# The last 512 tokens' sends to their expert slots: eight in a row behind one tile, or two behind each of four tiles

## The chip, the cores and the metric

The kernel runs on one core of one Trainium2 chip. The metric is device time in microseconds (us) of one execution, as the median of several. The names of the engines are those of the profile: PE is TensorE, PEld its weight loads, DVE is VectorE, ACT is ScalarE, POOL is GpSimd, SP is SyncE, and SPq is the queue on which SP issues its DMAs.

## The reference

One transformer block over 2048 tokens of width 128, in float32:

```python
h = _layernorm(x) * (1 + ca) + sa
x = x + ga * attention(h)      # 16 query heads, 4 key/value heads of 64, rotary, causal softmax
h = _layernorm(x) * (1 + cb) + sb
x = x + gb * ffn(h)            # 8 experts, 128 -> 512 -> 128, silu(g) * u; the top 2 of 8 for each token
```

The reference computes all eight experts for every token and weighs them with `tok_w`, which is zero but for two of them. The kernel computes only the two that count, so it has to sort tokens by expert.

## The kernel before, in words

Attention fills most of the time. It runs over four key/value groups; each handles the 16 token tiles (128 tokens each) in four chunks of 512 tokens. Then comes the expert stage, the only one that the change touches.

**Slots.** Every token has two rows to be computed, one per chosen expert. Each row is sent to a place in the DRAM tensor `sent`, so that each *slot tile* of 128 rows belongs to one expert. There are 40 slot tiles (`SLOT_TILES`), k = 0 to 39. They are fetched four at a time, as *quads* 0 to 9.

**Two batches of tokens.** The first 12 token tiles (`EARLY`) are ready while attention on the last chunk still runs; their 24 sends go out then, and they fill slot tiles 0 to 15 (`EARLY_SLOTS` is 16). The last four token tiles, 512 tokens, come late: their attention output is normalised, routed and counted between slot tiles 0 and 8 (the `late(k)` steps on PE and DVE), and DVE writes their places, `slot_of`, at slot tile 8 and signals `slots_ready`. Their rows may land in any slot tile from 16 on. A send is one indirect DMA of 128 rows issued by POOL; a token tile has two, one for each choice, so the late batch has eight.

**The work on one slot tile k.** PE does `gate_up(k)` (six matmuls, L1460). ACT takes silu of one half (L839), DVE multiplies it with the other (L1250). PE transposes the product, `turn_hidden(k)` (L1471), ACT copies it out (L832), and PE does `down(k)` (eight matmuls, L1482). DVE weighs the result, `y_out(k)` (L1218), which signals `y_copied`, and POOL writes it to the DRAM tensor `made` with one indirect DMA, `send_back(k)` (L681). PE's order within step k is `gate_up(k)`, `down(k-2)`, `turn_hidden(k-1)`; DVE's is the product of k, then `y_out(k-2)`; POOL's step k begins with `send_back(k-2)`. All queues are in order.

**A new quad.** SP fetches quad q (L549) once the buffer is free. Quad 4, the first that can hold late rows, has one more wait, for all sends to have landed:

```python
if q == EARLY_SLOTS // TB:
    sp.wait_ge(scattered, 2 * TILES * 16)
fetch(q)
```

Then PE transposes the quad (`turn_rows(q)`, L1448), ACT scales and rounds it (L823, L825), POOL computes the low parts (`split_rows(q)`, L675), and only then can PE start `gate_up` on its first tile. For quads 1, 2, 3 and 5 to 9 this begins two or three slot tiles ahead of need. Quad 4 alone is turned in step 15, directly ahead of slot tile 16.

**POOL's order** around the change is steps 8 to 15 of one loop. The sends of the late batch stand in step 10 (`LATE_SEND`), behind `send_back(8)`, all eight ahead of `send_back(9)`; `split_rows(4)` stands in step 15, behind `send_back(13)`.

Of the kernel before, what the change touches and what calls it, by code (L numbers as in the profile page):

```python
# [63 lines left out]
def block_kernel(nc, x_in, Wq, bq, Wk, bk, Wv, bv, Wo, bo, gate, w1, w2, w3, c, wmod,  # L64
# [5 lines left out]
    TILES = T // P  # L70
# [12 lines left out]
    EARLY, EARLY_LOWS = TILES - TB, 3  # L83
# [7 lines left out]
    def weight(x):  # L91

        if x[0] in ("s", "max"):
            _, J, m, t, b = x if x[0] == "max" else (x[0], x[1], x[4], x[3], x[2])
            part = 1.0 if b < J % N_J // PAIRS else ((t + 1) if x[0] == "max" else (TB - t)) / TB
            return part * (3.78 if x[0] == "max" else 2.0)
        if x[0] == "gap":
            return x[1]
        return {"pv": 2.1, "qmax": 1.5, "proj": 3.0, "low": 3.0, "qk": 3.5, "poolsum": 0.01, "maxed": 0.25,
                "diagsum": 3.3, "quadsum": 0.01, "sum": 2.8, "rowsum": 12.6, "norm": 2.8, "modulation": 0.0,  # L100
                "out": 8.0, "ln_stats": 1.0, "ln_scale": 1.0, "ln_turn": 2.0, "router": 4.0, "count": 4.0, "send": 1.0,
                "weights": 1.0}[x[0]]
# [63 lines left out]
    def merge(*placed):  # L166
        return [x for _, x in sorted((y for items in placed for y in items), key=lambda y: y[0])]
# [55 lines left out]
    for g in range(GROUPS):  # L223
        order = group_order(*(next_group if g < GROUPS - 1 else last_pair))
        at = [(p + g * begin[end], x) for (p, _), x in zip(order, of_group([x for _, x in order], g))]
        placed.append(at)
# [51 lines left out]
    with ExitStack() as ctx:  # L278
# [211 lines left out]
        def quad_turn(k):  # L490

            if k == EARLY_SLOTS - 1:
                return EARLY_SLOTS // TB
            q = k // TB + 1
            return q if k % TB == 1 and q < QUADS_OF_SLOTS and q != EARLY_SLOTS // TB else None
# [5 lines left out]
        LATE_OUT, LATE_TURN, LATE_ROUTER, LATE_COUNT, LATE_SEND = 0, 3, 4, 7, 10  # L501
# [75 lines left out]
        def _(pool):  # L577
# [78 lines left out]
            def send(t):  # L656
                late = t >= EARLY
                pool.wait_ge(slots_ready, 1 + late)
                pool.wait_ge(cleared, 16)
                tiles, rows = BATCH[late]  # L660
                for choice in range(2):
                    nc.gpsimd.indirect_dma_start(sent.ap(), bass.IndirectOffsetOnAxis(ap=slot_of[:, choice, t:t + 1], axis=0),  # L662
                                                 rows[:, t - tiles[0], :], None).then_inc(scattered, 16)
# [8 lines left out]
            def split_rows(q):  # L672
                width = len(quad_tiles(q)) * P
                pool.wait_ge(x_rounded, q + 1)
                nc.gpsimd.tensor_tensor(h_parts[:, q % 2, 1, 0:width], hT_full[:, q % 2, 0:width],  # L675
                                        h_parts[:, q % 2, 0, 0:width].bitcast(F32), ALU.subtract).then_inc(x_split, 1)

            def send_back(k):
                pool.wait_ge(y_copied, k + 1)
                pool.wait_ge(back_ready, k // TB + 1)  # L680
                nc.gpsimd.indirect_dma_start(made.ap(), bass.IndirectOffsetOnAxis(ap=back_to[:, k:k + 1], axis=0),  # L681
                                             y_rows[:, k % Y_ROWS, :], None).then_inc(written[k % Y_ROWS], 16)

            split_rows(0)
            for k in range(SLOT_TILES):
                if k >= 2:
                    send_back(k - 2)
                if k == LATE_SEND:
                    for t in range(EARLY, TILES):
                        send(t)  # L690
                if quad_turn(k) is not None:
                    split_rows(quad_turn(k))
            send_back(SLOT_TILES - 2)
# [868 lines left out]
```

## Time and profile before

| what | value |
|---|---|
| time, median of 3 | 1218.36 us (1216.64 to 1220.63) |
| the profiled execution: its own time | 1220.18 us |
| the profiled execution: its span | 1218.3 us |
| mean granted TensorE clock | 0.96 |
| PE busy | 1094.7 us, 90% of the span |
| DVE, POOL, ACT busy | 855.2 us (70%), 602.5 us (49%), 552.7 us (45%) |
| expert stage, first `gate_up` to the end of the span | about 1060 to 1218.3 us |

Positions are counted in microseconds from the start of the span. The span leaves out 1.9 us of the profiled execution's own time. The expert stage is the last 158 us; the stretch at issue lies between 1100 and 1130 us.

### The profile page before, as it was taken

The numbers are of one execution on the slowest core, as the hardware profiler recorded it, in microseconds if no ns is written. First come the engines' busy times: TensorE is split into PE (matmuls) and PEld (weight loads), VectorE is DVE, ScalarE is ACT, GpSimd is POOL, SyncE is SP. The second block draws the span as 40 slices with busy tenths as digits, with TensorE's granted clock in tenths as the row PEclk, the third lists the DMA queues.
The fourth block names the chain that finished last, engine by engine and source line by source line (L and its number), as shares of the span: only waits on it lengthen the run. The fifth ranks groups of instructions, "written<-read, shape, count | busy, mean of one in ns | idle before, by whom it ended". The sixth has DMA issues, their size and how long they took to land.

```text
span 1218.3 us, 16645 instructions
## 1 busy us (share of the span) xinstructions
PE 1094.7 (90%) x5718; PEld 660.7 (54%) x5718; DVE 855.2 (70%) x1751; ACT 552.7 (45%) x1156; POOL 602.5 (49%) x645
## 2 busy tenths in 40 slices
PE   2589999999999999999999999999999897287993
PEld 2355555554565655545656555556555443276893
DVE  3657878777779787777787877677877784664333
ACT  1344444545455445444454454535544344153451
POOL 2743655746346456453465554454555238325341
PEclk9699999999999999999999999999999898589997
DMA  9000000000000000000000000000100010502104
GB/s 240 1 1 1 1 2 1 1 1 1 1 2 1 1 1 1 1 1 1 1 1 1 1 1 1 1 1 1 70 1 1 1 48 32 148 14 75 33 24 119
DMA packets 32209, 25.28 MB, mean 21 GB/s; under 512 B 8448, under 2 KB 27264, under 8 KB 32128
## 3 DMA queue, kind: packets, MB, share of 16 engines
q1 hardware_dynamic: 22528, 17.08, 4.8%
q0 software_dynamic: 2304, 4.79, 1.2%
q10 hardware_dynamic: 7296, 2.36, 0.9%
q8 instruction: 47, 0.77, 0.3%
q14 instruction: 34, 0.28, 0.1%
HBM read 15.68 MB, written 8.54 MB: 20 GB/s over the span
## 4 chain that ended last, share of the span: by engine, by line
PE 71%; DVE 10%; issue 7%; POOL 6%; DMA 3%; ACT 2%; ACTq 1%; SPq 1%; POOLq 0%; DVEq 0%
PE PS L1386 18%; PE PS L1340 12%; PE PS L1368 10%; PE PS L1370 9%; PE PS L1460 4%; PE PS L1316 3%; DVE part_max L984 3%; PE PS L1482 2%; PE PS L1422 2%; PE PS L1353 2%; PE PS L1323 2%; PE PS L1396 2%; POOL sent L662 2%; DVE full L1000 1%; POOL full L616 1%
## 5 line engine op out<-in xcount | busy, mean ns | idle before, releaser
L984 DVE TENSOR_REDUCE part_max<-PS 128x1 f32<-128x512 f32 (+2 forms) x576 | 340.2, 618 | 135.1 <-PE PS L1340 111.2
L764 ACT ACTIVATE full<-PS 128x512 f32<-128x512 f32 x384 | 223.4, 598 | 196.6 <-PE PS L1370 185.5
L1368 PE MATMUL PS<-store 128*128 128x512 f32 (+3 forms) x640 | 273.6, 428 | 10.7 <-ACT full L764 7.2
L1340 PE MATMUL PS<-store 128*128 128x512 f32 (+3 forms) x640 | 249.6, 416 | 2.4 <-DVE V L965 1.3
L1370 PE MATMUL PS<-store 128*128 128x512 f32 (+3 forms) x640 | 234.8, 367 | 0.0
L616 POOL TENSOR_TENSOR full<-full 128x512 f32<-128x512 f32 x128 | 164.2, 1314 | 137.0 <-PE PS L1386 136.0
L773 ACT ACTIVATE diag<-PS 128x512 f32<-128x512 f32 (+3 forms) x256 | 111.3, 441 | 211.2 <-PE PS L1373 179.3
L644 POOL TENSOR_TENSOR lower<-lower 128x320 f32<-128x320 f32 x64 | 60.2, 941 | 275.1 <-DVE lower L962 272.8
L1340 PEld LDWEIGHTS PS<-store 128*128 128x128 f32 x640 | 119.1, 192 | 138.0 <-DVE part_max L984 59.6
L1386 PE MATMUL PS<-full,V 128*64 128x512 f32 x768 | 191.3, 608 | 0.0
L1368 PEld LDWEIGHTS PS<-store 128*128 128x128 f32 x640 | 123.5, 193 | 86.1 <-ACT full L764 28.4
L625 POOL TENSOR_TENSOR full<-full,diag 128x512 f32<-128x512 f32 (+3 forms) x128 | 108.8, 888 | 58.8 <-ACT diag L773 52.5
L1370 PEld LDWEIGHTS PS<-store 128*128 128x128 f32 x640 | 122.2, 191 | 13.2
L744 ACT ACTIVATE store<-PS 128x512 fp32r<-128x512 f32 (+1 forms) x192 | 92.9, 533 | 77.9 <-PE PS L1353 50.4
L1386 PE MATMUL PS<-diag,V 128*64 128x256 f32 (+3 forms) x512 | 96.6, 458 | 0.0
L1386 PEld LDWEIGHTS PS<-full,V 128*64 128x64 f32 x768 | 46.0, 137 | 67.8 <-issue 66.1
L1250 DVE TENSOR_TENSOR full<-full,PS 128x512 f32<-128x512 f32 x40 | 27.5, 687 | 70.3 <-ACT full L839 69.9
L1460 PE MATMUL PS<-store 128*128 x240 | 69.8, 429 | 7.7 <-issue 7.7
L649 POOL TENSOR_TENSOR lower<-lower 128x160 f32<-128x160 f32 x128 | 76.1, 615 | 0.0
L1029 DVE TENSOR_TENSOR full<-full 128x512 f32<-128x512 f32 x96 | 74.4, 780 | 0.0
L681 POOL DMA_INDIRECT made<-attnT,back_to x40 | 38.7, 966 | 66.8 <-DVE attnT L1218 65.9
L651 POOL TENSOR_TENSOR lower<-lower 128x320 f32<-128x320 f32 x64 | 63.1, 986 | 5.0
(211 smaller groups left out, 1505.3 us busy)
## 6 DMA issues: line engine op xcount, KB each, us to landing
lower<-in_L_ffn_experts_w_dram SPq DMA_DIRECT2D x16, 256.0 KB, 3.9
sent<-full SPq DMA_DIRECT2D x1, 2640.0 KB, 19.9
full<-sent SPq DMA_DIRECT2D x10, 264.0 KB, 4.0
lower<-made SPq DMA_DIRECT2D x8, 256.0 KB, 4.8
out_dram<-XA SPq DMA_DIRECT2D x4, 256.0 KB, 2.8
made<-attnT,back_to POOLq DMA_INDIRECT x40, 2.2
lower<-in_L_attn_Wq_dram ACTq DMA_DIRECT2D x1, 512.0 KB, 4.6
lower<-in_L_attn_bq_dram ACTq DMA_DIRECT2D x1, 512.0 KB, 9.7
```

The costliest lines, as they stand in the source:

```text
L616: last = nc.gpsimd.tensor_tensor(full[:, a, r], full[:, a, r], full[:, b, r], ALU.add)
L625: last = nc.gpsimd.tensor_tensor(acc[:, r, r * P:BANK], acc[:, r, r * P:BANK], diag[:, m, r, r * P:BANK], ALU.add)
L649: done = link(nc.gpsimd.tensor_tensor(rs[:, :, lo:hi], qk[:, :, HALF - lo:HEAD - lo], sn, ALU.mult))
L744: nc.scalar.activation(dst, src, ACT.Copy).then_inc(ring_act, 1)
L764: nc.scalar.activation(full[:, k % QUADS, r, :], PS[:, bank, :], ACT.Exp).then_inc(probs_ready, 1)
L773: nc.scalar.activation(diag[:, m, r, r * P:BANK], PS[:, bank, r * P:BANK], ACT.Exp)\
L984: nc.vector.reduce_max(part_max[:, t, b:b + 1], PS[:, bank, 0:width], AX.X).then_inc(ring_dve, 1)
L1340: last = nc.tensor.matmul(PS[:, bank, 0:w], QT[:, ch % 2, h, t * P:(t + 1) * P], KT[:, 0, keys:keys + w], start=True, stop=not last_bank)
L1368: nc.tensor.matmul(o, KT[:, 0, keys:keys + P], QT[:, ch % 2, h, q0:BANK], start=True, stop=False)
L1370: last = nc.tensor.matmul(o, KT[:, 1, keys:keys + P], QMT[:, h, q0:BANK], start=False, stop=q < ch)
L1386: last = nc.tensor.matmul(PS[HEAD * m:HEAD * (m + 1), AV + J % 2, q0:BANK], V[:, values(J // N_J * TILES + kt), :], pT, start=(kt == 0), s ...
L1460: last = nc.tensor.matmul(PS[:, bank + w, :], h_parts[:, q % 2, a, j * P:(j + 1) * P], parts_of[:, bass.ds(e, 1), w, part, :].rearrange("p ...
```

## The change

In POOL's loop over the slot tiles the eight late sends no longer go out together in step 10. Step 10 issues the two sends of token tile 12, step 11 those of 13, step 12 those of 14, step 13 those of 15. Each pair stands behind that step's `send_back`, which waits for `y_copied` of slot tile 8, 9, 10 and 11 in turn. `LATE_SEND` stays 10, `TILES` is 16 and `EARLY` is 12. Nothing else moves.

```diff
             for k in range(SLOT_TILES):
                 if k >= 2:
                     send_back(k - 2)
-                if k == LATE_SEND:
-                    for t in range(EARLY, TILES):
-                        send(t)
+                if k - LATE_SEND in range(TILES - EARLY):
+                    send(EARLY + k - LATE_SEND)
                 if quad_turn(k) is not None:
                     split_rows(quad_turn(k))
```

## Rows read from the trace of the kernel before

**Rows 1.** The page: busy us, share of the span, instructions.

```profile
PE 1094.7 (90%) x5718; PEld 660.7 (54%) x5718; DVE 855.2 (70%) x1751; ACT 552.7 (45%) x1156; POOL 602.5 (49%) x645
```

**Rows 2.** Chain that ended last, in order of time: start us, us, what.

```profile
1109.91 3.56 issue
1113.47 1.15 PE PS L1482 x8
1115.14 3.27 PE PS L1460 x6
...
1123.95 0.44 PE PS L1448 x4
1124.38 3.74 issue
1128.13 2.61 PE PS L1460 x6
```

**Rows 3.** Windows: stretch, us, each engine's busy us, clock, DMA share, GB/s.

```profile
1132.40:1180.00 47.60, 47.60 (x322) 43.35 (x321) 17.86 (x50) 25.09 (x42) 21.49 (x21) 1.00 0.10 30
```

**Rows 4.** Timeline of POOL, 1102 to 1128 us: start, us, what, [idle before].

```profile
1102.77 1.12 POOL L681 DMA_INDIRECT made<-attnT,back_to  x1 [0.39 <-DVE attnT L1218]
1104.20 0.96 POOL L662 DMA_INDIRECT sent<-full,slot_of  x1 [0.30 <-issue]
1105.46 0.97 POOL L662 DMA_INDIRECT sent<-full,slot_of  x1 [0.30 <-issue]
...
1113.05 0.96 POOL L662 DMA_INDIRECT sent<-full,slot_of  x1 [0.30 <-issue]
1114.32 0.95 POOL L681 DMA_INDIRECT made<-attnT,back_to  x1 [0.30 <-issue]
1115.58 0.96 POOL L681 DMA_INDIRECT made<-attnT,back_to  x1 [0.30 <-issue]
1120.28 0.96 POOL L681 DMA_INDIRECT made<-attnT,back_to  x1 [3.75 <-DVE attnT L1218]
```

**Rows 5.** Timeline of SP's queue from 1110 us.

```profile
1115.41 21.39 SPq L549 DMA_DIRECT2D full<-sent  x6
```

**Rows 6.** Line L549, the fetches of quads, from issue to landing.

```profile
DMA to landing us min/median/max: 2.6/4.0/5.4
```

**Rows 7.** Timeline of all engines, 1105 to 1120 us.

```profile
1106.32 0.34 DVE L1218 SCALAR_TENSOR_TENSOR attnT<-PS,V,gates 128x128 f32<-128x128 f32 x1
1106.91 1.15 PE L1482 MATMUL PS<-diag,full 128*128 x8 [0.63 <-issue]
1107.90 0.60 PE L1471 MATMUL PS<-ident,full 128*128 128x128 f32 x4
1108.26 1.65 PE L1460 MATMUL PS<-store 128*128 x6
1111.33 0.35 DVE L1218 SCALAR_TENSOR_TENSOR attnT<-PS,V,gates 128x128 f32<-128x128 f32 x1 [3.67 <-remote]
1112.75 0.58 ACT L832 COPY full<-PS 128x512 f32<-128x512 f32 x1 [5.80 <-remote]
1118.43 0.60 ACT L839 ACTIVATE full<-PS 128x512 f32<-128x512 f32 x1 [5.09 <-PE PS L1460]
1119.66 0.34 DVE L1218 SCALAR_TENSOR_TENSOR attnT<-PS,V,gates 128x128 f32<-128x128 f32 x1
```

**Rows 8.** Timeline of PE and ACT in the early batch's sends, 1007 to 1010 us.

```profile
1007.68 0.63 PE L1370 MATMUL PS<-store 128*128 128x512 f32 x1
1008.35 0.60 ACT L764 ACTIVATE full<-PS 128x512 f32<-128x512 f32 x1 [0.45 <-PE PS L1370]
1008.54 0.63 PE L1370 MATMUL PS<-store 128*128 128x512 f32 x1
1009.21 0.60 ACT L764 ACTIVATE full<-PS 128x512 f32<-128x512 f32 x1 [0.26 <-PE PS L1370]
```

**Rows 9.** Timeline: the first quad's turn, PE cold before it.

```profile
1054.91 1.09 PE L1448 MATMUL PS<-ident,full 128*128 128x128 f32 x4 [3.71 <-DMA full<-sent]
...
1059.98 2.92 PE L1460 MATMUL PS<-store 128*128 x6 [3.98 <-issue]
```

## Prediction

> **What bounds the kernel now.** I read the page first: PE is busy 90% of the span [rows 1]. Then the chain that ended last, from 1100 us on. From 1128.13 us, where `gate_up(16)` starts [rows 2], PE is busy without a gap: 47.60 of 47.60 us in the stretch from 1132.4 to 1180 us [rows 3]. Nothing behind slot tile 16 waits for anything else, so the end of the kernel moves one for one with the start of `gate_up(16)`. That start is the quantity to forecast.
>
> Ahead of it the chain has three holes [rows 2]: 3.56 us from 1109.91, a `gate_up(14)` of 3.27 us, and 3.74 us from 1124.38. The last one is the way of quad 4 from PE's turn through ACT and POOL back to PE: from the turn at 1123.95 (its record in the timeline is 0.17 us earlier) to 1128.13, which is 4.2 to 4.35 us. The turn itself did not wait for the fetch: it follows the work before it without idle time.
>
> The first hole needs the timelines. PE ran `down(10)` at 1106.91 and `turn_hidden(11)` at 1107.90; their ends by the record are 1108.06 and 1108.50. But `y_out(10)` on DVE, which waits for the first, started at 1111.33, and the copy on ACT, which waits for the second, at 1112.75. `gate_up(13)` ended at 1109.91, and its silu started at 1118.43 [rows 7]. PE's results reached their readers 3.3, 4.2 and 8.5 us late. These *late answers* lie inside the stretch in which POOL issued indirect DMAs without a pause, 1102.77 to 1116.54: `send_back(8)`, eight sends, `send_back(9)` and `send_back(10)`, one every 1.26 us [rows 4]. They end at 1118.4, 1.9 us behind POOL's last. The eighteen sends of the early batch, at the same spacing, had no such effect: ACT starts 0.04 us behind PE's ends there [rows 8]. So the run of DMAs goes with the late answers in one place and not in the other; I can't name the mechanism.
>
> The Trainium skill (Perfetto Trace Analysis, section Tensor Engine Instruction) says that the end of a matmul in a profile is worked out from its size, while the signal goes out once PSUM has confirmed the writes. By that rule the lateness could sit inside PE's writes rather than in the signal. The sum would be the same by either, since both count from the reader's start.
>
> **The change part by part.** No instruction is added or removed; the work of eight sends and of all `send_back`s is the same, and DVE, ACT and PE are untouched.
>
> *Moved earlier:* `send_back(9)` from 1114.32 to at best 1106.73, and (10) from behind the burst too. Nobody waits for them: their buffer is written again eight tiles later. Worth nothing.
>
> *Moved later:* sends 3 to 8. The last send now has three more DMAs ahead of it, `send_back(9)`, (10) and (11). At 1.26 us each [rows 4] that is 3.79 us: from 1113.05 to 1116.84 at the earliest. Four steps now hold three DMAs each, 3.79 us, which is more than PE's 2.7 us for a slot tile in steady state (322 PE instructions in 47.60 us, 18 matmuls a tile), so pairs don't give POOL any pause while PE is on time: POOL is as dense as before.
>
> *The new wait:* the last pair stands behind `send_back(11)`, thus behind `y_out(11)`. Queued behind it are SP's fetch of quad 4 (and 5 to 7 behind that), and `split_rows(4)`. In the profile `y_out(11)` ended at 1120.00 [rows 7], since its step's silu was the one held up to 1118.43. Before the change this lateness touched PE alone; now it also holds the sends.
>
> From the end T of `y_out(11)`: 0.28 us to `send_back(11)` (1120.00 to 1120.28) [rows 4, 7], two times 1.26 us to the last send's start, 2.36 us from there to the fetch (1113.05 to 1115.41) [rows 4, 5], the fetch 2.6 to 4.0 us (shortest and median; I take 3.3) [rows 6], then 4.35 us from turn to `gate_up(16)`; after a longer idle PE it may be 5.07 us, as with quad 0 (1054.91 to 1059.98) [rows 9]. So `gate_up(16)` starts at T + 0.28 + 2.53 + 2.36 + 3.3 + 4.35 = T + 12.8. Before it was 1128.13. Break-even is T = 1115.3. The slack ahead of that: before, quad 4 was in by about 1118.7 and turned at 1123.8, so 5.1 us of delay cost nothing.
>
> The Trainium skill (DMA: Bandwidth & Descriptors, section Anatomy of one DMA) gives a DMA from POOL about 2.0 us plus its bytes over 436 GB/s. For 128 rows of 528 bytes that would be an estimated 2.16 us where the trace has 2.36, and the sum would be 0.2 us shorter.
>
> The bounds of T. Lowest: POOL's own pace, `send_back(11)` at 1114.32, an effective T of 1114.04. Highest: as before, 1120.00. In between: the first six DMAs from 1102.77 keep their times whatever the order, so the first late answer stays, and `y_out(10)` ends at 1111.68. Now POOL has to wait for it (its last send before that ended at about 1110.2), which it did not before. It then issues `send_back(10)` and two sends, from 1111.72 to 1115.2. If answers come 1.9 us behind the end of the run, as before, silu(13) starts at 1117.1 instead of 1118.43, and T is 1.57 us behind it (1118.43 to 1120.00): 1118.65.
>
> **Likeliest: the late answers stay, a bit shorter; chance 0.40.** T = 1118.65 gives 1131.45, 3.3 us later than before. On the profiled execution that is 1220.2 + 3.3 = 1223.5 us; that execution lies 1.8 us above the median of the runs shown, and I add the change to the median: 1218.36 + 3.3 = 1221.7 us. Its own range is 1219.8 to 1223.5 (T 1.5 us less, or the fetch 0.7 and the turn 0.7 us longer).
>
> **Rivals.**
> *A, the pairs end the late answers; 0.20.* For it: they were there only beside eight sends in a row. Against: the spacing on POOL stays 1.26 us. PE is then early and the sends are what it waits for: 1116.84 + 2.36 + 3.3 + 4.35 = 1126.85, up to 1127.6 with a cold PE. Gain 0.5 to 1.3 us: 1217.1 to 1217.9 us. No case gives more, as POOL's pace is the floor; a shortest fetch adds 0.7 us.
>
> *B, the slack covers the delay; 0.12.* T falls between 1114 and 1115.3, the fetch lands before PE comes to the turn at 1123.8: 1218.4 us, no change.
>
> *C, the late answers are as long as before; 0.13.* T = 1120.00, and `gate_up(16)` starts at 1132.8: 4.7 us later, 5.4 with a cold PE: 1223.0 to 1223.8 us, slower by over 0.3%. It decides from T = 1119.0 up. For it: nothing in the change takes a DMA away. Against: POOL now pauses for `y_out(10)`.
>
> *D, the late answers are not in the timed executions; 0.15.* They may be rare or belong to the profiled execution. Then before the fetch landed at 1115.41 + 3.3 = 1118.7 with PE waiting for it, and `gate_up(16)` began at 1123.1; after the change 1126.85. The three `send_back`s in front cost their full 3.8 us: 1222.2 us. The runs shown spread over 4.0 us, about the 5 us between a start at 1123.1 and one at 1128.1, which leaves room for this.
>
> **How the numbers follow.** About 0.3%, 3.7 us, is what can be told from no change. The likeliest case lies just inside it (3.3 us), and about 4 in 10 of it beyond; C lies beyond for most, D for half, A and B within. Slower: 0.40 x 0.4 + 0.13 x 0.9 + 0.15 x 0.5, about 0.35; with the nearness of the bound and the scatter of medians 0.38. Faster: only A with luck of the medians, 0.05. Same: 0.57. The range takes A's middle at its low end and C's high end: 1217.0 to 1224.2; the likeliest case's own is above.
>
> **What would show it.** On POOL's timeline: `send_back`, send, send four times from 1102.8, the last send's start at 1116.8 (A, D), near 1121.5 (likeliest) or 1122.8 (C). SP's first fetch after 1110 us 2.4 us behind it, against 1115.41. PE at the turn of quad 4 (L1448 near 1124 to 1127) idle with the DMA named as its releaser, where before there was no idle time. On ACT a silu (L839) with some 4 us of idle before it near 1117: if all gaps are under 1 us, the late answers are gone. Behind `gate_up(16)` nothing should change.
>
> The prediction is wrong if the late answers grow (they may depend on something else than POOL's run, the fetches for instance, which now fall later), if a fetch behind the sends is slower than 4.0 us, or if the kernel ends earlier by more than 2 us, for which the trace shows no room.

## The result, and the profile after

The changed kernel is slower: ratio 1.0036 with a 95% interval of 1.0025 to 1.0047, which is 4.4 us (3.0 to 5.7). Its median is 1220.18 us over 20 executions (1218.12 to 1226.90), against 1215.97 us over 20 executions of the kernel before (1213.76 to 1220.63); the medians differ by 4.2 us. A change in us stands for the ratio's distance from 1 times the median of before, here and in the experiments. The forecast was 1221.7 us in a range of 1217.0 to 1224.2, a change of 3.3 us. The time lies in the range. The change lies just beyond the 0.3% that I had set as the bound of "same" (which I had given more chance, 0.57, than "slower", 0.38), and, as it turned out, it did not come by the way I had called likeliest.

In the changed kernel POOL issues what was expected, `send_back`, send, send, four times. Its timeline (start us, us, what, [idle before]):

```profile
1106.97 1.12 POOL L681 DMA_INDIRECT made<-attnT,back_to  x1 [0.39 <-DVE attnT L1217]
1108.39 0.96 POOL L662 DMA_INDIRECT sent<-full,slot_of  x1 [0.31 <-issue]
1109.66 0.97 POOL L662 DMA_INDIRECT sent<-full,slot_of  x1 [0.30 <-issue]
1111.13 0.96 POOL L681 DMA_INDIRECT made<-attnT,back_to  x1 [0.51 <-DVE attnT L1217]
...
1118.71 0.96 POOL L681 DMA_INDIRECT made<-attnT,back_to  x1 [0.30 <-DVE attnT L1217]
1119.97 0.96 POOL L662 DMA_INDIRECT sent<-full,slot_of  x1 [0.30 <-issue]
1121.24 0.96 POOL L662 DMA_INDIRECT sent<-full,slot_of  x1 [0.30 <-issue]
```

From `send_back(8)` to the last send it is now 14.27 us, where it was 10.28 us (1102.77 to 1113.05, [rows 4]). The chain that ended last shows what hangs on it (start us, us, what):

```profile
1121.24 2.28 DMA sent<-full,slot_of
...
1123.59 2.75 DMA full<-sent
1126.34 0.04 issue
1126.39 1.11 PE PS L1447 x4
1127.50 3.70 issue
1131.20 2.92 PE PS L1459 x6
```

Last send, landing, fetch of quad 4, its turn on PE, the way through ACT and POOL, `gate_up(16)`. (The edit has one line less, so the numbers of the lines behind it are lower by one.) PE now waits for the fetch; before, in the first profile, the turn followed other PE work. Timeline of PE in the changed kernel:

```profile
1120.27 0.60 PE L1470 MATMUL PS<-ident,full 128*128 128x128 f32 x4
1126.39 1.11 PE L1447 MATMUL PS<-ident,full 128*128 128x128 f32 x4 [5.52 <-DMA full<-sent]
1131.20 2.92 PE L1459 MATMUL PS<-store 128*128 x6 [3.70 <-issue]
```

And the late answers are gone. ACT's timeline, silu (L838) of slot tiles 10 and 13 to 16:

```profile
1105.11 0.60 ACT L838 ACTIVATE full<-PS 128x512 f32<-128x512 f32 x1
...
1114.12 0.60 ACT L838 ACTIVATE full<-PS 128x512 f32<-128x512 f32 x1 [0.81 <-PE PS L1459]
...
1116.85 0.60 ACT L838 ACTIVATE full<-PS 128x512 f32<-128x512 f32 x1 [0.81 <-PE PS L1459]
...
1119.57 0.60 ACT L838 ACTIVATE full<-PS 128x512 f32<-128x512 f32 x1 [0.81 <-PE PS L1459]
...
1134.16 0.60 ACT L838 ACTIVATE full<-PS 128x512 f32<-128x512 f32 x1 [5.17 <-PE PS L1459]
```

So two readings of the result were open. The first profile of before has 29.86 us from silu(10) to silu(16), with the late answers in it:

```profile
1100.91 0.60 ACT L839 ACTIVATE full<-PS 128x512 f32<-128x512 f32 x1
...
1130.77 0.60 ACT L839 ACTIVATE full<-PS 128x512 f32<-128x512 f32 x1 [4.86 <-PE PS L1460]
```

The profile after has 29.05 us (1105.11 to 1134.16) without them: by these two executions alone the stretch got shorter by 0.8 us, while the timed executions say 4.4 us longer. The spans can't decide it, since they hold differences from far ahead of the change (silu(10) itself is 4.2 us later in the profile after than in the one before). From here on "the stretch" is the time from silu(10) to silu(16); both ends are starts on ACT.

### The profile page after: what moved, and what is told of

Read it like the earlier page. It is cut to its first block, busy times and chain, and to the rows that moved or that the text cites. A ratio compares the mean times of both kernels' runs of the same rounds, so it can differ in the third digit from the quotient of the medians.

```text
span 1222.5 us, 16645 instructions
## 1 busy us (share of the span) xinstructions
PE 1096.7 (90%) x5718; PEld 662.3 (54%) x5718; DVE 856.0 (70%) x1751; ACT 553.5 (45%) x1156; POOL 602.6 (49%) x645
## 3 DMA queue, kind: packets, MB, share of 16 engines
q10 hardware_dynamic: 7296, 2.36, 0.8%
## 4 chain that ended last, share of the span: by engine, by line
PE 69%; DVE 11%; issue 7%; POOL 6%; DMA 3%; ACT 2%; ACTq 1%; SPq 0%; POOLq 0%; DVEq 0%
PE PS L1385 18%; PE PS L1339 12%; PE PS L1367 10%; PE PS L1369 9%; PE PS L1459 3%; DVE part_max L983 3%; PE PS L1315 3%; PE PS L1421 2%; DVE full L999 2%; PE PS L1352 2%; PE PS L1322 2%; PE PS L1395 2%; PE PS L1481 2%; POOL sent L662 2%; PE PS L1342 1%
```

## The experiments

Each kernel was timed against the kernel before in five rounds, unless said otherwise. "Order theory" is rival D of the prediction: the time goes with what POOL issues ahead of the last send. "Late-answer theory" and "wait theory" are the two parts of what I had thought likeliest: PE's results reach their readers late, and so the last pair of sends is held by the result of slot tile 11.

**1. The kernel before again** (no edit).

> The kernel before once more, timed against itself and with a second profile. Both theories: ratio 1.000, within 0.2%. Order theory (the late answers between 1108 and 1118 us in the first profile are an accident of that execution): in this profile no silu (L839) between slot tiles 8 and 15 has more than 1 us of idle time before it, and PE waits for the fetch of quad 4 before its turn, some 2 to 3 us. Late-answer theory (they belong to eight sends in a row): they are there again, 3 to 8 us each, and the turn of quad 4 has no idle time before it.

Ratio 0.9994 (0.9979 to 1.0009). There are no late answers in its profile. Timeline of ACT, silu of slot tiles 10, 13 and 16:

```profile
1099.66 0.60 ACT L839 ACTIVATE full<-PS 128x512 f32<-128x512 f32 x1
...
1108.67 0.60 ACT L839 ACTIVATE full<-PS 128x512 f32<-128x512 f32 x1 [0.80 <-PE PS L1460]
...
1124.28 0.60 ACT L839 ACTIVATE full<-PS 128x512 f32<-128x512 f32 x1 [5.16 <-PE PS L1460]
```

The stretch is 24.62 us, 5.2 us shorter than in the first profile. Timeline of PE: without late answers PE is early, and it waits for the fetch in the kernel before too.

```profile
1114.78 0.60 PE L1471 MATMUL PS<-ident,full 128*128 128x128 f32 x4
1116.98 0.66 PE L1448 MATMUL PS<-ident,full 128*128 128x128 f32 x4 [1.60 <-DMA full<-sent]
1121.33 2.92 PE L1460 MATMUL PS<-store 128*128 x6 [3.69 <-issue]
```

The 5.1 us of slack that I had read from the first profile does not exist here: a delay of the last send should go straight to `gate_up(16)`, which experiments 3 and 6 try. (The wait is 1.6 us, where the expectation had 2 to 3.)

**2. The waits alone.**

```diff
                 if k == LATE_SEND:
                     for t in range(EARLY, TILES):
+                        pool.wait_ge(y_copied, t - EARLY + LATE_SEND - 1)
                         send(t)
```

> All eight sends stay ahead of send_back(9), but the pairs wait for the results of slot tiles 8, 9, 10 and 11 as they do in the changed kernel. Order theory (the three send_backs that now stand ahead of the last send cost 3.8 us, and the waits nothing, since each result is there when POOL comes to it): within 0.1% of the kernel before. Wait theory (the last pair is held by the result of slot tile 11, which comes late): slower by 3 to 5 us, as the changed kernel.

Ratio 1.0001 (0.9987 to 1.0014), stretch 24.92 us, 0.3 us more than in experiment 1. One of the waits shows: 0.2 us at the result of slot tile 9. Timeline of POOL:

```profile
1107.34 0.97 POOL L662 DMA_INDIRECT sent<-full,slot_of  x1 [0.30 <-issue]
1108.82 0.95 POOL L662 DMA_INDIRECT sent<-full,slot_of  x1 [0.51 <-DVE attnT L1219]
...
1115.13 0.95 POOL L662 DMA_INDIRECT sent<-full,slot_of  x1 [0.31 <-issue]
1116.39 0.96 POOL L681 DMA_INDIRECT made<-attnT,back_to  x1 [0.30 <-DVE attnT L1219]
```

The changed kernel has the same 0.51 us of idle time at its `send_back(9)`. The waits on four results do not carry the loss.

**3. Four and four:** one `send_back` ahead of the last send in place of three.

```diff
-                if k == LATE_SEND:
-                    for t in range(EARLY, TILES):
+                if k in (LATE_SEND, LATE_SEND + 1):
+                    for t in range(EARLY + 2 * (k - LATE_SEND), EARLY + 2 * (k - LATE_SEND) + 2):
                         send(t)
```

> Four sends behind send_back(8), four behind send_back(9): one DMA more ahead of the last send, where the changed kernel has three. Order theory: 1.26 us slower than before, 0.10%. Wait theory: the last four wait for the result of slot tile 9 alone, which is there in time: no change. Burst theory (eight in a row do harm by themselves): faster than before.

Ratio 1.0010 (0.9996 to 1.0025). The timing fits the 1.26 us and does not exclude zero; it excludes a net gain of over 0.04% from breaking up the row of eight. The profile resolves it: last send 13.39 us behind silu(10), against 12.14 in experiment 1; stretch 26.44 us, 1.8 us more. The 0.5 us beyond the DMA is the turn on PE:

```profile
1118.96 1.11 PE L1448 MATMUL PS<-ident,full 128*128 128x128 f32 x4 [2.88 <-DMA full<-sent]
```

It takes 1.11 us here against 0.66 in experiment 1, behind 2.88 us of idle time.

**4. The sends ahead of `send_back(8)`:** one DMA less ahead of the last send.

```diff
-                if k >= 2:
-                    send_back(k - 2)
                 if k == LATE_SEND:
                     for t in range(EARLY, TILES):
                         send(t)
+                if k >= 2:
+                    send_back(k - 2)
```

> The eight sends ahead of send_back(8) in step 10 instead of behind it: one DMA less ahead of the last send. Order theory: the last send 1.3 to 1.7 us earlier (POOL is free some 0.4 us before the result of slot tile 8), and the kernel 1.3 to 1.7 us faster, 0.10 to 0.14%, so long as PE waits for the fetch of quad 4. If the fetch is hidden behind PE's own work, as the first profile has it: no change.

Ratio 0.9998 (0.9982 to 1.0014). The interval, 2.2 us faster to 1.7 us slower, leaves room for the 1.3 to 1.7 us that I expected, so the timing alone decides nothing. The profile shows the miss. The last send did come 1.66 us earlier (10.48 us behind silu(10)), but the stretch is 24.13 us, only 0.5 shorter. Timeline of POOL, the last of six `send_back`s in a row and `split_rows(4)`:

```profile
1112.13 0.96 POOL L681 DMA_INDIRECT made<-attnT,back_to  x1 [0.30 <-issue]
...
1117.18 0.96 POOL L681 DMA_INDIRECT made<-attnT,back_to  x1 [0.30 <-issue]
1118.44 0.96 POOL L681 DMA_INDIRECT made<-attnT,back_to  x1 [0.30 <-issue]
1119.42 1.27 POOL L675 TENSOR_TENSOR store<-full,store 128x512 fp32r<-128x512 f32 x1
```

ACT had its rounding, on which the split waits, done at 1118.17 (start 1117.40, 0.77 us). The split started at 1119.42, since six `send_back`s, held up by the sends, stood ahead of it. What the earlier sends won, POOL's backlog took back. This new wait is tested below.

**5. The changed kernel again** (no edit to it).

> The changed kernel once more, with a second profile. Slower than before by 3.8 to 4.4 us, 0.31 to 0.36%. Order theory: from silu(10) to silu(16) on ACT 29.0 us as in the first profile of it (24.6 in the second profile of before), last send 4.0 us later than there counted from silu(10), no late answers. If the first profile of it was a lucky one, late answers show up and the stretch is 31 us or more.

Ratio 1.0035 (1.0024 to 1.0045), stretch 29.17 us (1101.24 to 1130.41), last send 16.13 us behind silu(10), no late answers. The result and the first profile after both repeat.

**6. All eight sends in step 13,** behind `send_back(11)`.

```diff
-                if k == LATE_SEND:
+                if k == LATE_SEND + 3:
                     for t in range(EARLY, TILES):
```

> All eight sends in a row, but in step 13 behind send_back(11): three send_backs ahead and the whole row behind the result of slot tile 11. Order theory: the last send 8.8 us later than before, counted from silu(10) (send_back(11) at 10.9, then eight times 1.26 us, against 12.14), and the kernel 8.8 to 9.5 us slower, 0.72 to 0.78%: the end moves one for one with the last send. If something else bounds the stretch as well: clearly less than that.

Ratio 1.0075 (1.0056 to 1.0094), 9.2 us. The last send starts 21.03 us behind silu(10), 8.9 us later than in experiment 1; the stretch is 34.07 us, 9.5 longer. Against experiment 1, the stretch has grown by as much as the last send is later, and half a microsecond more, in experiments 3, 5 and 6 alike (1.8 for 1.3, 4.6 for 4.0, 9.5 for 8.9 us).

**7. The sends in step 9,** where `slot_of` has just been written.

```diff
             for k in range(SLOT_TILES):
+                if k == LATE_SEND - 1:
+                    send(EARLY)
+                    split_rows(quad_turn(k))
+                    for t in range(EARLY + 1, TILES):
+                        send(t)
                 if k >= 2:
                     send_back(k - 2)
-                if k == LATE_SEND:
-                    for t in range(EARLY, TILES):
-                        send(t)
-                if quad_turn(k) is not None:
+                if k != LATE_SEND - 1 and quad_turn(k) is not None:
                     split_rows(quad_turn(k))
```

> Two sends ahead of split_rows(3) and six behind it in step 9, with send_back(7) behind them all. Order theory: the last send 4 us earlier than before, the fetch of quad 4 landed before PE comes to its turn, so PE's own work bounds, 2 us sooner; but POOL has seven send_backs left ahead of split_rows(4), which takes back up to 1 us, as with the sends ahead of send_back(8), where this backlog held split_rows(4) by 1.2 us. Sum: 1 to 2.5 us faster, 0.1 to 0.2%. If the backlog on POOL is no bound: 2.5 to 3 us faster.

Ratio 0.9976 (0.9962 to 0.9991), 2.9 us faster. The last send is 7.95 us behind silu(10), 4.2 us earlier than in experiment 1, and the stretch 22.11 us, 2.5 shorter: the fetch is hidden now, since PE has no idle time ahead of the turn, and the rest of the 4.2 us has nothing left to win. Of the 2.5 us, `gate_up(16)` starting earlier is 1.7; the other 0.8 is `gate_up(16)` itself, 2.13 us here against 2.92 in experiment 1. The backlog that I had feared did not hold the split: it started at 1117.64, 0.08 us behind the end of ACT's rounding.

**8. The turn of quad 4 in step 14 as well.**

```diff
-            if k == EARLY_SLOTS - 1:
+            if k == EARLY_SLOTS - 2:
                 return EARLY_SLOTS // TB
```

> As the kernel with the sends in step 9, and quad 4 is turned in step 14 instead of 15, split_rows(4) behind send_back(12). Order theory: one send_back less ahead of split_rows(4), and PE does gate_up(15), down(13) and turn_hidden(14) in the time in which it waited for the split: a further 1 us, 2 to 4 us faster than before in all, 0.2 to 0.3%. If PE waits in step 14 for the fetch for longer than it saves later: no gain over the kernel with the sends in step 9.

Ratio 0.9954 (0.9939 to 0.9970), 5.6 us faster (4.5 us by the medians). Stretch 20.34 us. In its profile `split_rows(4)` stands behind a backlog again, six `send_back`s, and PE has 1.67 us of idle time ahead of `gate_up(16)`. Timelines of PE (first) and POOL of this kernel:

```profile
1121.76 0.60 PE L1473 MATMUL PS<-ident,full 128*128 128x128 f32 x4
1124.03 1.63 PE L1462 MATMUL PS<-store 128*128 x6 [1.67 <-issue]
```

```profile
1120.90 0.95 POOL L681 DMA_INDIRECT made<-attnT,back_to  x1 [0.30 <-issue]
1121.87 1.28 POOL L675 TENSOR_TENSOR store<-full,store 128x512 fp32r<-128x512 f32 x1
```

**9. Experiment 4 with the split first:** `split_rows(4)` ahead of `send_back(13)`.

```diff
+                if quad_turn(k) == EARLY_SLOTS // TB:
+                    split_rows(quad_turn(k))
                 if k >= 2:
                     send_back(k - 2)
-                if quad_turn(k) is not None:
+                if quad_turn(k) not in (None, EARLY_SLOTS // TB):
                     split_rows(quad_turn(k))
```

> The eight sends ahead of send_back(8), as before, and split_rows(4) ahead of send_back(13) in step 15. Backlog theory (in the kernel with the sends ahead of send_back(8), five send_backs in a row held split_rows(4) and took back what the earlier sends had won): split_rows(4) starts 1.2 us sooner after the turn, the stretch from silu(10) to silu(16) is 22.9 us against 24.1 there and 24.6 before, and the kernel is 1.5 to 1.7 us faster than before, 0.12 to 0.14%. If the earlier sends are worth nothing for another reason: 24.1 us again.

Ratio 0.9981 (0.9970 to 0.9992), 2.3 us faster than before (1.4 us by the medians). Stretch 23.03 us, against 24.13 in experiment 4 with the last send at the same 10.48 us behind silu(10). The backlog theory (the row of `send_back`s held the split) holds: it explains 1.1 of the 1.2 us that were missing there.

**10. Experiment 8 with the same edit,** so `split_rows(4)` ahead of `send_back(12)`.

> The kernel with the sends in step 9 and the turn in step 14, and split_rows(4) ahead of send_back(12). Backlog theory: split_rows(4) starts 1.2 us sooner, and PE's wait of 1.67 us ahead of gate_up(16) falls to some 0.5 us: silu(10) to silu(16) 19.1 us against 20.3, the kernel 1.2 us faster than that one, 5.5 to 7 us faster than before, 0.45 to 0.57%. If PE's wait was for something else: 20.3 us again.

Ratio 0.9942 (0.9929 to 0.9956), 7.1 us faster than before (the medians, 1209.62 against 1215.79 us in the same rounds, say 6.2): the version that beats both kernels by most. Stretch 19.17 us. Timeline of PE: the idle time ahead of `gate_up(16)` is 0.46 us, and the turn and `gate_up(16)` run without a drop of the clock.

```profile
1115.96 0.66 PE L1452 MATMUL PS<-ident,full 128*128 128x128 f32 x4
1116.89 1.65 PE L1464 MATMUL PS<-store 128*128 x6 [0.27 <-issue]
...
1120.32 1.64 PE L1464 MATMUL PS<-store 128*128 x6 [0.46 <-issue]
```

In experiment 1 `gate_up(16)` stands behind 3.69 us of idle time and takes 2.92 us. The windows of `gate_up(16)` there and here show the 1.2 and the 2.4 GHz level:

```profile
1121.33:1124.25 2.92, 2.92 (x7) 2.34 (x8) 0.00 (x0) 0.00 (x0) 0.00 (x0) 0.50 0.00 0
```

```profile
1120.32:1121.96 1.64, 1.64 (x8) 1.40 (x9) 0.00 (x0) 0.17 (x1) 1.24 (x2) 1.00 0.12 40
```

So 1.3 of the 5.5 us by which the stretch is shorter than in experiment 1 is the clock, which comes back with the idle time gone. The low clock also lasts beyond the stretch: silu(17) starts 4.30 and 2.91 us behind silu(16) in experiments 1 and 11, both the kernel before, and 2.71 us behind it in experiments 8 and 10. Counted to silu(17), experiment 10 is 5.7 to 7.0 us shorter than the kernel before, which is what the timing shows.

**11. The kernel before, a third profile** (one execution, not timed in rounds).

> A third profile of the kernel before, for the late answers alone. If they are rare: none, silu(10) to silu(16) 24.6 us. If they come in every second or third execution of it: a fair chance of a stretch near 30 us.

No late answers: stretch 24.62 us (1106.53 to 1131.15), to the hundredth that of experiment 1. This execution took 1220.12 us all the same, since its silu(10) was 6.9 us later than there. A long execution is no sign of late answers.

## Why the prediction was right, and where it was not

**What bounds the kernel** was right: the end follows `gate_up(16)`. That the last send sets that start, experiments 3, 5 and 6 show in steps of 1.3, 4.0 and 8.9 us. "One for one" leaves something out: the low clock at `gate_up(16)` lasts for a different time in each execution. From silu(16) to silu(17) it is 4.30 and 2.91 us in experiments 1 and 11, 4.02 and 3.30 us in the two profiles of the changed kernel, so two executions of one kernel differ by up to 1.4 us there.

**"The three `send_back`s in front cost their full 3.8 us"** (rival D, 0.15) is what happened. From experiment 1 to the first profile of the changed kernel the stretch got longer by 4.43 us (24.62 to 29.05):

- three DMAs at 1.26 us, 3.79 us, as in the prediction;
- 0.20 us for the result of slot tile 9, which POOL now reaches 0.2 us too early. I had costed the new waits at zero for a POOL that is never ahead of PE; experiment 2 shows the same 0.20 us without the `send_back`s;
- 0.45 us for the turn of quad 4, 1.11 us in place of 0.66. It is the clock: PE had been idle for 5.52 us, and the windows (us, busy us of each engine, granted clock, DMA share, GB/s) show 0.50, the 1.2 GHz level, in the changed kernel:

```profile
1126.30:1127.50 1.20, 1.11 (x4) 0.71 (x4) 0.66 (x4) 0.00 (x0) 0.00 (x0) 0.50 1.03 309
```

and 1.00, the 2.4 GHz level, behind 1.60 us of idle time in experiment 1:

```profile
1116.98:1117.64 0.66, 0.66 (x4) 0.42 (x4) 0.56 (x4) 0.00 (x0) 0.66 (x1) 1.00 1.05 322
```

I had kept this as the "cold PE", with 0.7 us, outside the sum. The three terms make 4.44 us, and the timed difference is 4.4 us (3.0 to 5.7). That they meet this closely is chance: counted to silu(17) the profiles of the changed kernel are 3.6 to 5.5 us longer than experiments 1 and 11.

**The step that failed: "Likeliest: the late answers stay, a bit shorter".** They were an event of one execution. Of thirteen profiles (three of before, two of after, eight variants) only the first has them. I took the only profile for the usual case, and from it read a slack of 5.1 us and a T of 1118.65. In the usual case there is no slack, PE waits for the fetch by 1.6 us, and T plays no part. That 3.3 us came out near 4.4 is luck: two errors against each other, counted from silu(10), a start of `gate_up(16)` 5.5 us too late before (27.22 for 21.67) and one 4.5 us too late after (30.54 for 26.09). The sign that I had at hand and gave too little weight: the early batch's sends beside PE and ACT without a late answer [rows 8]. They were not all "at the same spacing", as the prediction has it: of the seventeen gaps between the eighteen starts ten are 1.26 or 1.27 us, the others 1.33 to 2.09. But the four rows shown lie in a row of six sends at 1.26 or 1.27 us.

**Rival A** (the pairs end the late answers, and the kernel gains 0.5 to 1.3 us) would have been confirmed by the two first profiles alone, 29.86 against 29.05 us. The timed executions and the second profile of before refute it. **B and C** both rest on the late answers and go with them: without them there was no slack to cover anything.

**The floor of POOL's pace** was right: the last send lies 14.27 us behind `send_back(8)` where I had 14.07. From the last send's start to SP's fetch I had 2.36 us; the profiles have 2.35 (1121.24 to 1123.59) and, in experiment 1, 2.36 (1111.80 to 1114.16). The Trainium skill's fit (DMA: Bandwidth & Descriptors, Anatomy of one DMA), an estimated 2.16 us for the DMA alone, is 0.2 us short of this distance, which runs on to SP's next issue; the sum goes by the measurement. For the fetch I had 3.3 us; it took 2.75.

**The base.** I added the change to the median of three executions, 1218.36 us; twenty gave 1215.97. The prediction (1221.7) was 1.5 us too high: 2.4 us too much there, less the 0.9 us by which the medians' difference of 4.2 us exceeds my 3.3.

**What stays open** is what the late answers are. The prediction's figures of them (3.3, 4.2 and 8.5 us) stand on the readers' starts in one execution; no later run had any, so no experiment could work on them, and they are neither tied to eight sends in a row nor cleared of it. I also did not try whether they occur in executions that are not profiled.

## What to carry to other kernels

Where a step's share of a queue is longer than the step itself (three DMAs of 1.26 us against 2.7 us of PE), spreading work over the steps does not thin the queue out; it only decides who comes last. Put first on the queue what somebody waits for (the sends, then the split), and last what nobody waits for (the write-backs): the same instructions gave from 9.2 us slower to, with one turn moved a step ahead, 7.1 us faster. Part of what a removed wait gives back is the clock: PE idle for 3.7 us came back at half speed. And a gap of a few microseconds that one execution shows is one sighting: work out the sum without it too, and before two kernels are compared by their profiles, take a second profile of each and a stretch that leaves out what lies far ahead.

## What the runs showed of the hardware

- PE's results reached their readers 3.3 to 8.5 us late, counted from the recorded ends, for 10 us of one execution out of thirteen profiled ones, while ACT's reached theirs on time (the product of slot tile 12 started within 0.1 us of its silu's end, `down(11)` 0.14 us behind the copy).
- An idle time of 2.88 us before the turn of quad 4 was followed by transposes at the lower clock (1.11 us for four, experiment 3; the granted clock of such a turn is 0.50 in the changed kernel), one of 1.60 us was not (0.66 us, experiment 1). It adds 0.45 us on top of a wait. `gate_up(16)` took 2.92 us at a granted clock of 0.50 behind 3.69 us of idle time and 1.64 us at 1.00 behind 0.46. Idle time alone doesn't fix the moment: in the first profile of before `down(11)` ran at 1.00 right behind 3.56 us of idle time, and only `gate_up(14)`, which started 1.4 us later, at 0.51 (2.91 us).
- Where POOL waits for nothing, indirect DMAs of 128 rows start 1.26 us apart, 0.96 of it the instruction, in this stretch of every kernel here, for sends and `send_back`s alike and for up to fourteen in a row.
